# A decoder's first phase: 64-row transposes issued right behind the scores, projected and memory keys side by side in one tensor, and two of four softmax scalings moved from ScalarE to GpSimd

## The chip, the cores and the metric

The kernel runs on one core of one Trainium2 chip. The metric is the time of one execution in microseconds (us). Three runs of the kernel before took 1528.6, 1529.95 and 1530.91 us; the median, 1529.95 us, is what the change is compared with. One execution is also taken with the hardware profiler. The engines are called as the profile calls them: PE is TensorE's matmuls, PEld its weight loads, DVE is VectorE, ACT is ScalarE, POOL is GpSimd, SP is SyncE.

## The reference, cut to what matters

Input `x` is (32, 128, 128) in float32: 32 sequences of 128 rows with 128 features. Six residual blocks follow one another: a recurrent attention with 16 heads of 8, a cross attention with 16 heads of 64, a mixture of 8 experts with the best 2 chosen, a causal attention with normalised queries and keys, a banded cross attention, and a quantised linear layer. The change touches the second block only. In short:

```python
q = layernorm(x) @ wq + bq          # 16 heads of 64
k = concat(ctx @ wk + bk, mk)       # 128 projected keys, 128 memory keys
v = concat(ctx @ wv + bv, mv)
attn = softmax(q @ k.T / 8)         # 128 x 256 for each head
x = x + (attn @ v) @ wo + bo
```

The memory keys `mk` and values `mv` are the same for all sequences.

## The kernel before, in words

The program has three phases, one after the other on all engines: the first computes the recurrent attention, the cross attention and the routing; the second the experts; the third the last three blocks. Each engine has its own in-order program, written out by hand, and engines wait for each other on counting semaphores (`wait_ge`).

**The first phase is staged in slots.** All five programs loop over a slot number `s` from -53 to 152. Sequences are worked on in 8 groups of 4 (512 columns). The cross attention is cut into 128 **units**, one a slot from slot 0 on: a unit is one sequence and four heads (`hq` says which four of the 16), and 16 units make a group. `unit(i)` gives group, four heads and sequence. What belongs to one unit is spread over five slots:

- slot s: PE computes the scores (lines 744 and 746), 128 queries by 256 keys for each of four heads, into two PSUM banks. Two heads lie on the partitions 0 to 63, two on 64 to 127; a matmul has 64 rows of weights (queries) and streams keys, 128 projected ones from `KT` (tensor `kt_w2`), then 128 memory keys from `mkT`. DVE takes the negated maximum of the four heads (line 1122). ACT exponentiates each head into `pr` and sums it (line 950).
- slot s+1: DVE takes the reciprocals of the sums (line 1096, counted in semaphore `b_nd` when it is through) and scales heads 0 and 1 of `pr` in place (line 1099); ACT scales heads 2 and 3 (line 925, counted in `b_na`).
- slot s+2 (`LAG_PT`): PE transposes the eight 128x128 blocks of `pr` through full 128-row transposes (line 760) into banks 4 and 5, four blocks a bank; ACT copies each bank to `ptS` (line 934).
- slot s+3 (`LAG_PV`): PE multiplies with the values (line 898), 64 output partitions a head.
- slot s+4 (`LAG_OT`): ACT copies the result to `aoT` (line 917).

A float32 matmul appears as two instructions of equal shape, a transpose as one.

**What else a slot holds.** Every slot computes a chunk of the projected queries or keys (lines 852 and 857, with ACT copies in lines 1017 and 1021), and either a chunk of values (line 868, added to its bias by DVE in line 1081) or a part of the output projection (line 880, added to the residual by DVE in line 1088). Both of the latter go to bank 4, which the transposes of the next slot overwrite; so those transposes wait for that DVE addition (semaphores `b_v`, `b_add`), and the chunk waits for ACT's copy of bank 4 (`b_pts`). Bank 7 is shared by the steps of the recurrent attention and of the routing, of which most slots have one (table `BANK7`).

**GpSimd's queue** does one product of 128x512 in each of the slots 1 to 96 (lines 664 and 670, `KV`), always after it has waited for `b_nd`, that is for DVE's scaling in the same slot; also additions and products (lines 675, 677, 688), powers for the layer norms (line 352), and the indirect stores of routed rows (line 702). **DVE's order in a slot**: addition for the value or output chunk of the slot before, reciprocal, scaling, in some slots a scan (line 1068), the maximum (line 1122), then the steps of the recurrent attention and of the routing, many of them with two operands in SBUF (lines 1139, 1160, 1197 to 1200, 1235, 1243, 1313), and a scan in most odd slots. **ACT's order**: copy to `aoT`, scaling of heads 2 and 3, two copies to `ptS`, four exponentials, copies out of bank 7, the copy of the chunk.

## Time and profile before

| | |
|---|---|
| median of three runs | 1529.95 us (1528.6 to 1530.91) |
| the profiled execution's own time | 1531.66 us |
| its span, first to last instruction | 1529.7 us |
| busy: PE, PEld | 1362.8 us (89%), 1040.4 us (68%) |
| busy: DVE, ACT, POOL | 1148.0 us (75%), 1099.5 us (72%), 597.9 us (39%) |
| mean granted TensorE clock | 0.977 of full speed |
| units of the cross attention | scores start at 131.1 us (first unit) and 812 us (last) |

The page is read from the span down: busy shares of the engines, the span in forty slices, the chain of work that ended last, and the costliest groups of instructions. PE is the busiest engine, and matmul ends are modelled, so its share alone says little; the times between starts of matmuls say more.

### The profile page before, as it was taken

Reading aid. Unit: us, or ns where it says so; the run is one execution under the profiler, and the core shown is the slowest. Engines: PE = TensorE matmul, PEld = TensorE weight load, DVE = VectorE, ACT = ScalarE, POOL = GpSimd, SP = SyncE. Lnnn points to the kernel's source line nnn. Section 1 sums busy time; section 2 is a strip of 40 time slices with the busy share of each in tenths; the row PEclk is TensorE's granted clock in tenths of the full one; section 3 lists DMA queues with packets and bytes.
Section 4 is the critical chain, followed back from the end, with each engine's and each line's share of the span. In section 5 each row is a group of like instructions: output and inputs, shape, how many; then the busy total and the mean of one; then the engine's idle time right before and its main releaser. Section 6 shows DMA issues by size and latency. Waiting matters only on the chain.

```text
span 1529.7 us, 42924 instructions
## 1 busy us (share of the span) xinstructions
PE 1362.8 (89%) x15465; PEld 1040.4 (68%) x15465; DVE 1148.0 (75%) x2779; ACT 1099.5 (72%) x2899; POOL 597.9 (39%) x679
## 2 busy tenths in 40 slices
PE   2258999999999999999997699979889999999995
PEld 0124777777777777777776699957667777777763
DVE  3899879898898989786655444457778888787765
ACT  1126998898898898899995366657667877767763
POOL 0002333344443524330202635346754755544552
PEclk9999999999999999999999799989999999999997
DMA  6644141321423231102011333240000110000000
GB/s 171 154 112 104 43 105 36 90 63 37 108 53 89 58 81 46 50 15 77 15 36 49 87 98 87 58 141 18 20 23 25 25 38 10 23 23 3 23 9 15
DMA packets 82317, 88.63 MB, mean 58 GB/s; under 512 B 15296, under 2 KB 71488, under 8 KB 77504
## 3 DMA queue, kind: packets, MB, share of 16 engines
q1 hardware_dynamic: 74496, 73.65, 18.7%
q0 software_dynamic: 4096, 8.40, 1.9%
q10 hardware_dynamic: 3520, 3.84, 0.8%
q8 instruction: 130, 2.13, 0.6%
q14 instruction: 75, 0.61, 0.1%
HBM read 64.89 MB, written 17.83 MB: 54 GB/s over the span
## 4 chain that ended last, share of the span: by engine, by line
PE 65%; DVE 24%; issue 5%; ACT 3%; DMA 2%; ACTq 1%; POOL 1%; SPq 0%; DVEq 0%; POOLq 0%
PE P L898 7%; PE P L760 7%; PE P L1985 6%; PE P L744 5%; PE P L1481 4%; PE P L1514 4%; PE P L880 3%; DVE xnE L2310 3%; PE P L746 3%; PE P L868 3%; DVE qS L2310 3%; PE P L857 3%; PE P L852 3%; PE P L2003 3%; PE P L1947 2%
## 5 line engine op out<-in xcount | busy, mean ns | idle before, releaser
L950 ACT ACTIVATE pr<-P,nm 128x256 f32<-128x256 f32 x512 | 237.7, 489 | 9.7 <-DVE nm L1122 9.7
L1122 DVE TENSOR_REDUCE nm<-P 128x4 f32<-128x1024 f32 x128 | 156.1, 1220 | 46.7 <-PE P L746 46.5
L2194 ACT ACTIVATE et<-P 128x1024 f32<-128x1024 f32 x128 | 131.2, 1025 | 59.2 <-PE P L1992 59.0
L352 POOL TENSOR_TENSOR rstd<-ve,mhalf 128x1 f32<-128x1 f32 (+2 forms) x81 | 75.5, 936 | 225.9 <-DVE ve L347 225.3
L934 ACT COPY ptS<-P 128x512 f32<-128x512 f32 x256 | 136.8, 586 | 31.2 <-PE P L760 30.7
L760 PE MATMUL P<-ident,pr 128*128 128x128 f32 x1024 | 140.2, 280 | 5.5 <-DVE xb L1088 3.0
L925 ACT ACTIVATE pr<-pr,ri 128x256 f32<-128x256 f32 x256 | 118.9, 523 | 27.9 <-DVE pr L1099 26.6
L744 PE MATMUL P<-kt_w,qt 64*128 64x128 f32 x1024 | 126.7, 309 | 2.9 <-ACT pr L950 2.7
L760 PEld LDWEIGHTS P<-ident,pr 128*128 128x128 f32 x1024 | 110.3, 141 | 21.9 <-issue 8.6
L1573 ACT ACTIVATE hT<-P,mixing 128x128 f32<-128x128 f32 x284 | 81.4, 369 | 60.5 <-PE P L1481 60.5
L664 POOL TENSOR_TENSOR kv_qk<-kv_qk,r_w 128x512 f32<-128x512 f32 x48 | 61.1, 1272 | 161.9 <-DVE pr L1099 115.7
L670 POOL TENSOR_TENSOR kv_qk<-kv_qk,mixing 128x512 f32<-128x512 f32 x48 | 61.1, 1273 | 154.1 <-DVE pr L1099 154.1
L746 PE MATMUL P<-mkT,qt 64*128 64x128 f32 x1024 | 113.9, 272 | 0.0
L2310 DVE TENSOR_REDUCE qS<-P 128x8 f32<-128x1024 f32 x64 | 78.2, 1222 | 46.8 <-PE P L1985 46.4
L950 ACT ACTIVATION_READ_ACCUMULATOR pr<-P,nm 128x1 f32 x512 | 112.9, 220 | 0.0
L744 PEld LDWEIGHTS P<-kt_w,qt 64*128 64x128 f32 x1024 | 91.7, 185 | 28.0 <-issue 26.0
L2310 DVE TENSOR_REDUCE xnE<-P 128x8 f32<-128x1024 f32 x64 | 78.4, 1225 | 40.3 <-PE P L1985 39.3
L898 PE MATMUL P<-ptS,V 128*64 128x128 f32 x1024 | 106.7, 287 | 0.0
L898 PE MATMUL P<-ptS,mv 128*64 128x128 f32 x1024 | 100.0, 274 | 0.0
L898 PEld LDWEIGHTS P<-ptS,V 128*64 128x64 f32 x1024 | 58.1, 137 | 55.3 <-issue 40.7
L1902 POOL TENSOR_SCALAR_AFFINE_SELECT et<-et 128x1024 f32<-128x1024 f32 x64 | 71.0, 1109 | 61.1 <-ACT et L2194 60.6
L746 PEld LDWEIGHTS P<-mkT,qt 64*128 64x128 f32 x1024 | 92.3, 188 | 0.0
(355 smaller groups left out, 3929.2 us busy)
## 6 DMA issues: line engine op xcount, KB each, us to landing
kv_qk<-scr_v SPq DMA_DIRECT2D x16, 1024.0 KB, 8.1
r_w<-scr_r SPq DMA_DIRECT2D x16, 1024.0 KB, 10.5
xt<-scr_xs SPq DMA_DIRECT2D x71, 64.0 KB, 1.8
scr_ys<-yt SPq DMA_DIRECT2D x71, 64.0 KB, 1.5
x<-in_x SPq DMA_DIRECT2D x8, 256.0 KB, 9.8
scr_v<-mixing SPq DMA_DIRECT2D x8, 256.0 KB, 2.0
scr_r<-mixing SPq DMA_DIRECT2D x8, 256.0 KB, 2.0
xb<-in_x SPq DMA_DIRECT2D x8, 256.0 KB, 4.3
```

The source lines that it names most:

```text
L744: nc.tensor.matmul(bank[:, cc * KEYS:cc * KEYS + T], q, KT[part, c, b * T:(b + 1) * T], start=True, stop=True)
L746: m = nc.tensor.matmul(bank[:, cc * KEYS + T:(cc + 1) * KEYS], q, mkT[part, c, :], start=True, stop=True)
L760: m = nc.tensor.transpose(P[:, 4 + kb, h * T:(h + 1) * T], pr[:, i % 3, h * KEYS + kb * T:h * KEYS + (kb + 1) * T], ident[:, :])
L898: m = nc.tensor.matmul(P[64 * hh:64 * hh + 64, 6, cc * T:(cc + 1) * T], src, ptS[:, i % 2, (kb * 4 + h) * T:(kb * 4 + h + 1) * T], start=( ...
L925: m = nc.scalar.activation(t, t, ACT.Copy, scale=ri[:, i % 3, h:h + 1])
L934: nc.scalar.copy(ptS[:, i % 2, kb * 512:(kb + 1) * 512], P[:, 4 + kb, :])\
L950: e = nc.scalar.activation(pr[:, s % 3, h * KEYS:(h + 1) * KEYS], scores(s)[:, h // 2, (h % 2) * KEYS:(h % 2 + 1) * KEYS], ACT.Exp, bias=n ...
L1122: nc.vector.tensor_reduce(nm[:, s % 3, 0:4].rearrange("p (a h) -> p a h", a=2), scores(s).rearrange("p a (h k) -> p a h k", k=KEYS), AX.X, ...
L1573: m = nc.scalar.activation(hT[:, t % 3, c, :], P[:, 2 + t % 2, c * 128:(c + 1) * 128], ACT.Gelu, bias=b1[:, bass.ds(e1 + c, 1)])
L1985: return nc.tensor.matmul(scores[:, k, a, :], q[part, a, cols], keys[part, a, cols], start=False, stop=(a == 3))
L2194: nc.scalar.activation(et[:, u % 4, :, :, :], scoresT, ACT.Exp).then_inc(S["h_exp"], 1)
L2310: nc.vector.tensor_reduce(q[:, b, :, DH].rearrange("p (a r k) -> p r k a", r=2, k=2)[:, r], scores, AX.X, ALU.max, negate=True).then_inc(S ...
```

## The change

Three things. The projected keys and the memory keys stand side by side in one tensor, 640 columns for each pair of heads, so that one matmul streams 256 columns through a strided pattern (the keys of sequence b and the memory keys). The transposes work on 64 partitions each, sixteen in place of eight, with a moving identity of 64 columns; the lower 64 queries go to bank 4, the upper ones to bank 5, and ACT's two copies write with a stride. The scaling of heads 2 and 3 moves from ACT's program to POOL's, ahead of the products, and waits there for `b_ri`, which DVE raises after head 0. The sizes of the other tensors and the number of DMAs stay as they were.

```diff
-        r8_w1, kt_w2, qt = [sb_shared(n, E * F) for n in ("r8_w1", "kt_w2", "qt")]
+        r8_w1, qt = [sb_shared(n, E * F) for n in ("r8_w1", "qt")]
+        kt_w2 = sb_shared("kt_w2", 8 * (N + MEM))
...
-            mkT = sb1("mkT", [128, 8, MEM])
...
-            KT = kt_w2.rearrange("p (c n) -> p c n", n=N)
+            KT = kt_w2.rearrange("p (c n) -> p c n", n=N + MEM)
+            mkT = KT[:, :, N:N + MEM]
...
@@ pool_program
                 for s in range(FIRST, LAST + 16):
+                    i = s - 1
+                    if 0 <= i < UNITS:
+                        pool.wait_ge(S["b_ri"], i + 1)
+                        for h in range(2, 4):
+                            t = pr[:, i % 3, h * KEYS:(h + 1) * KEYS]
+                            m = nc.gpsimd.tensor_scalar(t, t, ri[:, i % 3, h:h + 1], None, ALU.mult)
+                        m.then_inc(S["b_na"], 1)
...
@@ tensor_program, scores
                             for hh in range(2):
-                                bank = scores(s)[:, hh, :]
                                 part, c = slice(64 * hh, 64 * hh + 64), 2 * hq + cc
-                                q = QT[part, c, b * T:(b + 1) * T]
-                                nc.tensor.matmul(bank[:, cc * KEYS:cc * KEYS + T], q, KT[part, c, b * T:(b + 1) * T],
-                                                 start=True, stop=True)
-                                m = nc.tensor.matmul(bank[:, cc * KEYS + T:(cc + 1) * KEYS], q, mkT[part, c, :],
-                                                     start=True, stop=True)
+                                keys = KT[part, c, :].rearrange("p (m k) -> p m k", k=T)[:, b:GS + 1:GS - b, :]
+                                m = nc.tensor.matmul(scores(s)[:, hh, cc * KEYS:(cc + 1) * KEYS], QT[part, c, b * T:(b + 1) * T],
+                                                     keys, start=True, stop=True)
                         m.then_inc(S["b_s"], 1)
...
@@ tensor_program, transposes
                         for kb in range(2):
                             for h in range(4):
-                                m = nc.tensor.transpose(P[:, 4 + kb, h * T:(h + 1) * T],
-                                                        pr[:, i % 3, h * KEYS + kb * T:h * KEYS + (kb + 1) * T],
-                                                        ident[:, :])
-                            m.then_inc(S["b_pt"], 1)
+                                k = 4 * kb + h
+                                for half in range(2):
+                                    part = slice(64 * half, 64 * half + 64)
+                                    m = nc.tensor.transpose(P[:, 4 + half, 64 * k:64 * k + 64],
+                                                            pr[part, i % 3, h * KEYS + kb * T:h * KEYS + (kb + 1) * T],
+                                                            ident[part, part])
+                                    if k == 7:
+                                        m.then_inc(S["b_pt"], 1)
...
@@ scalar_program
-                    i = s - 1
-                    if 0 <= i < UNITS:
-                        act.wait_ge(S["b_ri"], i + 1)
-                        for h in range(2, 4):
-                            t = pr[:, i % 3, h * KEYS:(h + 1) * KEYS]
-                            m = nc.scalar.activation(t, t, ACT.Copy, scale=ri[:, i % 3, h:h + 1])
-                        m.then_inc(S["b_na"], 1)
...
-                        for kb in range(2):
-                            act.wait_ge(S["b_pt"], 2 * i + kb + 1)
-                            nc.scalar.copy(ptS[:, i % 2, kb * 512:(kb + 1) * 512], P[:, 4 + kb, :])\
-                              .then_inc(S["b_pts"], 1)
+                        for half in range(2):
+                            act.wait_ge(S["b_pt"], 2 * i + half + 1)
+                            nc.scalar.copy(ptS[:, i % 2, :].rearrange("p (k q) -> p k q", q=T)[:, :, 64 * half:64 * half + 64],
+                                           P[:, 4 + half, :].rearrange("p (k q) -> p k q", q=64)).then_inc(S["b_pts"], 1)
```

## Rows read from the trace of the kernel before

**Rows 1.** Stretches: length; PE, PEld, DVE, ACT, POOL busy; clock; DMA share, GB/s.

```profile
484.23:574.41 90.18, 89.38 (x816) 67.11 (x814) 77.88 (x180) 80.33 (x239) 35.75 (x29) 1.00 0.27 69
...
574.41:661.96 87.55, 85.57 (x805) 65.06 (x803) 73.71 (x173) 76.47 (x233) 33.32 (x27) 1.00 0.16 41
...
661.96:745.38 83.42, 83.42 (x795) 64.01 (x793) 59.39 (x155) 75.60 (x230) 12.67 (x12) 1.00 0.15 43
```

**Rows 2.** PE's waits, 130 to 818 us: total, times, longest.

```profile
PE P L760 <- DVE xb L1088: 3.0, 4, 1.7
...
PE P L744 <- ACT pr L950: 2.7, 3, 1.4
```

**Rows 3.** PE's timeline through one slot: start, length, what, count.

```profile
672.34 0.50 PE L744 MATMUL P<-kt_w,qt 64*128 64x128 f32 x4
...
673.11 0.49 PE L746 MATMUL P<-mkT,qt 64*128 64x128 f32 x4
...
673.54 1.09 PE L760 MATMUL P<-ident,pr 128*128 128x128 f32 x8
...
674.47 1.02 PE L857 MATMUL P<-xTb,wq 128*128 128x512 f32 x2
...
675.33 1.05 PE L880 MATMUL P<-wo,aoT 128*128 128x128 f32 x8
...
677.33 0.39 PE L744 MATMUL P<-kt_w,qt 64*128 64x128 f32 x2
```

**Rows 4.** PE's timeline where matmuls stream 8 columns only.

```profile
721.46 0.96 PE L825 MATMUL P<-rw,tT 128*128 128x8 f32 x8
```

**Rows 5.** PEld's timeline, same slot: output projection's first load.

```profile
674.92 0.19 PEld L880 LDWEIGHTS P<-wo,aoT 128*128 128x128 f32 x1 [0.26 <-ACT ptS L934]
```

**Rows 6.** By line and shape, 110 to 800 us: busy, mean ns.

```profile
L925 ACT ACTIVATE pr<-pr,ri 128x256 f32<-128x256 f32 x244 | 113.4, 524 | 26.2 <-DVE pr L1099 24.8
...
L1180 DVE TENSOR_REDUCE hn<-r_w 128x64 f32<-128x512 f32 x7 | 4.7, 676 | 0.0
```

**Rows 7.** DVE's waits, 484.3 to 574.4 us: first and last of six.

```profile
DVE nm L1122 <- PE P L746: 6.1, 8, 1.1
...
DVE ri L1096 <- ACT pr L950: 0.2, 1, 0.2
```

**Rows 8.** DVE's waits, 495.47 to 545.80 us, both of them.

```profile
DVE nm L1122 <- PE P L746: 0.8, 1, 0.8
...
DVE xb L1206 <- PE P L804: 0.6, 1, 0.6
```

**Rows 9.** DVE's, then POOL's timeline in a slot of that stretch.

```profile
513.61 0.62 DVE L1099 TENSOR_SCALAR pr<-pr,ri 128x256 f32<-128x256 f32 x2
...
514.14 1.22 DVE L1122 TENSOR_REDUCE nm<-P 128x4 f32<-128x1024 f32 x1
...
515.28 0.85 DVE L1197 TENSOR_TENSOR r_w<-r_w,gnw 128x512 f32<-128x512 f32 x1
...
516.16 0.69 DVE L1198 TENSOR_TENSOR r_w<-r_w,gnb 128x512 f32<-128x512 f32 x1
...
514.32 1.27 POOL L670 TENSOR_TENSOR kv_qk<-kv_qk,mixing 128x512 f32<-128x512 f32 x1 [2.15 <-DVE pr L1099]
```

**Rows 10.** DVE's, then POOL's timeline in an earlier slot.

```profile
192.44 1.63 DVE L1099 TENSOR_SCALAR pr<-pr,ri 128x256 f32<-128x256 f32 x2
...
192.51 1.41 POOL L688 TENSOR_TENSOR xb<-xb,bias 128x512 f32<-128x512 f32 x1
```

**Rows 11.** POOL's instructions by line and shape, whole run.

```profile
L1902 POOL TENSOR_SCALAR_AFFINE_SELECT et<-et 128x1024 f32<-128x1024 f32 x64 | 71.0, 1109 | 61.1 <-ACT et L2194 60.6
...
L1897 POOL TENSOR_SCALAR_AFFINE_SELECT et<-et 128x512 f32<-128x512 f32 x64 | 43.2, 674 | 78.7 <-ACT et L2194 78.1
...
L1924 POOL COPY vE<-ctk 128x128 f32<-128x128 f32 x32 | 9.8, 308 | 0.0
...
L670 POOL TENSOR_TENSOR kv_qk<-kv_qk,mixing 128x512 f32<-128x512 f32 x48 | 61.1, 1273 | 154.1 <-DVE pr L1099 154.1
```

More of the change, by code:

```diff
@@ L647, in sync_program @@
                             e0, e1 = half * E // 2, (half + 1) * E // 2
-                            sp.dma_start(units_of(kt_w2)[:, e0 * FC:e1 * FC, :],
+                            sp.dma_start(units_of(kt_w2[:, 0:E * F])[:, e0 * FC:e1 * FC, :],
                                          d["w2T"].rearrange("(u f) h -> f u h", f=128)[:, e0 * FC:e1 * FC, :])\
@@ L1016, in scalar_program @@
                             act.wait_ge(S["b_kp"], 8 * g + c + 1)
-                            nc.scalar.activation(KT[:, c, :], P[:, 3, :], ACT.Identity, bias=bqk[:, 1, c:c + 1])\
+                            nc.scalar.activation(KT[:, c, 0:N], P[:, 3, :], ACT.Identity, bias=bqk[:, 1, c:c + 1])\
                               .then_inc(S["b_k"], 1)
@@ L1349, in sb2 @@
                 return own.enter_context(nc.sbuf_tensor(name, shape, dt))
-            w1, w2, b1, b2 = r8_w1, kt_w2, mixing[:, 0:E * D], mixing[:, 8 * N:8 * N + E * D]
+            w1, w2, b1, b2 = r8_w1, kt_w2[:, 0:E * F], mixing[:, 0:E * D], mixing[:, 8 * N:8 * N + E * D]
             qS, kS, vD, xb, ya, yb, xnD, xTd, qkv, qkq, hn3 = homes
```

## The prediction

> **What bounds the kernel now.** I read the windows first, one for each group of sixteen slots. A steady group takes 90.2 us with PE busy 89.4, ACT 80.3, DVE 77.9 and POOL 35.8, at the full clock [rows 1]; the last groups with less side work keep PE as full and leave DVE idle. PE's waits come next: while the 128 units run, its matmuls wait little, most of it for DVE's addition out of bank 4 (3.0 us) and for ACT's exponentials (2.7 us) [rows 2]. So PE's own stream paces most slots. The timeline of one slot says what it is made of: 4.99 us from scores to scores, 1.20 of it from the first score to the first transpose, 0.93 the eight transposes, 0.86 a chunk of two 512-column instructions [rows 3]. Last, DVE's waits: in a steady group they total 9.6 us [rows 7], but in the nine slots from 495.47 to 545.80 us only 1.4 us [rows 8]. There DVE is a second bound, close under PE, and what is added to it there is paid in time.
>
> **The change, part by part.** The sum is made against the profiled execution's 1531.66 us, 1.7 above the median, and carried over to the median as it is.
>
> *Scores.* Sixteen instructions of 128 columns become eight of 256. They run two at a time, on the two halves of the rows, as the counts and lengths show: sixteen starts in 1.20 us, while a stream of 512 columns takes 0.43, so one of 128 takes 0.107 and sixteen in a row would take 1.71 [rows 3]. The streaming is the same 0.86 after the change (four times 0.215). Now the last score starts 0.99 after the first (673.60, where the last group ends, less 0.27, the length of one) and streams until 1.10. After: 0.1 for the first weight load, then 0.86 and 0.01 of offset, 0.97. That is 0.12 less; nothing less is the other bound, since the same columns flow.
>
> *Transposes.* Eight pairs of 64-row transposes with 64 moving columns stream half as long, but each still loads 128 columns of weights. The price of such a load shows where matmuls stream only 8 columns: eight starts within 0.96 less 0.25 of length, hence one every 0.11 us although nothing is streamed [rows 4]. Pairs of loads run side by side in the scores. So eight pairs take 8 x 0.11, what eight transposes take today; only the last one's stream is shorter, 0.05. Between scores and transposes PE idles today some 0.15 (1.20 less 1.10, and the second transpose late); after, the rows of scores and transposes match, but the chunk behind them uses all 128, so I move the gap and credit nothing. The Trainium skill, "TensorEngine Tiling (Array Packing)", section Key Properties, says that changing the tiling mode drains the engine; by that rule too the number of drains a slot is unchanged. The same page, section Theoretical Speedup, gives up to 2x for a dimension of 64 or less; that would be 0.44 a slot and is a rival below.
>
> Both together: **0.17 us a slot**, bounds 0.05 and 0.32 (the gap gone as well).
>
> *Two halves complete together.* ACT's first copy starts after the fourth transpose today and after the last pair then, 0.44 later; 0.27 is given back because the transposes begin that much earlier (0.12 and the gap), 0.05 by the shorter stream. PE's load for the output projection waited for that copy until 674.92, 0.4 before its matmul at 675.33 [rows 3, 5]. It moves to 675.04 and the matmul to 675.16: just in time, so zero, covered by the 0.86 of the chunk. If ACT were late, every microsecond would show.
>
> *ACT* loses two activations a slot, 2 x 0.52 [rows 6]. It was not the bound: zero. Its earlier exponentials may give back part of the 2.7 that PE waits for exponentials [rows 2]; I take none, the end is -2.7. The strided writes of the copies move as many elements: zero. SP's program issues the same DMAs.
>
> *POOL* gets two scalings of 128x256 in each slot, in front of its product and in front of everything else of that slot. One-source operations cost 0.67 for 512 and 1.11 for 1024 elements, a copy of 128 costs 0.31; the two-source product 1.27 for 512 [rows 11]. The two sizes make 0.24 to start and 0.22 for 256 elements, 0.46; from the copy it is 0.31 + 0.11 = 0.42. I take **p = 0.43**, nearer the copy, the closest in length; the ends are 0.34 (half of the 0.67) and 0.72 (the two-source product, 0.64 in proportion, with a start). The Trainium skill, "GPSIMD Engine Reference", section Elementwise — side-by-side cycle accounting, gives 1.8 cycles an element as the best case of a loop of several operations; by that figure, as an estimate, a scaling would be 0.38 and a start, 0.62, and the sum that of the slower rival. PE needs the scaled heads a slot later, some 4 us. POOL is busy 2.2 us of 5.6 a slot [rows 1] and 3.1 then, so that wait costs nothing. The new wait, on `b_ri`, ends before today's wait on `b_nd`, so what is queued behind it (the product, powers, indirect stores) is held up by the two scalings alone.
>
> *But POOL and DVE block each other.* In a tight slot POOL's product ends at 515.59, and DVE's product with two SBUF operands, begun at 515.28, takes 0.85 where the equal one behind it takes 0.69 [rows 9]. In an earlier slot one of two scalings on DVE, 0.62 together elsewhere, waits out POOL's addition: 1.63 [rows 10]. The maximum, which reads PSUM, runs beside POOL at its 1.22. Today the product starts right behind DVE's scaling and lies almost wholly under that maximum; only 0.16 sticks out. Afterwards two scalings come first. The start of the first is hidden behind DVE's scaling (0.14, as in that earlier slot, where 1.41 less 0.28 of waiting leaves 1.13 for a 1.27), so the product ends 2p - 0.30 = **0.56 later**, and a DVE instruction with two SBUF operands or a scaling behind the maximum waits that much longer. The Trainium skill, "SBUF — State Buffer", section Who interferes with whom, calls this an exclusive lock held for the whole instruction; the trace agrees, 0.85 against 0.69.
>
> In the nine tight slots two have a 0.68 reduction [rows 6] behind the maximum, which needs no lock: free. Seven pay 0.56, 3.9 in all. DVE has 1.4 of waits there to absorb, and about 0.4 of lateness at either end. So the stretch, 50.3 us, grows by **2.1**. In the other seven slots DVE waits over 1 us each and PE's gain holds: -1.2. A steady group: **+0.9**.
>
> **The sum.** Four steady groups +3.6. The first, and the one at 574 us where DVE is 4 us less busy [rows 1], half way between the full gain of -2.7 and +0.9: -0.9 each, -1.8. The 31 slots from 662 us on, where POOL has no products and DVE idles: 31 x 0.17 = -5.3. Total -3.5: 1531.66 becomes 1528.2, and the median 1529.95 becomes **1526.4**. PE gains some 21 us, of which DVE takes 18 back.
>
> **The rivals.**
>
> *The block costs nothing extra* (products slip into later gaps, or POOL scales in well under 0.4): 127 x 0.17 = 21.6, less about 2 that DVE cannot follow in the tight slots: -19, 1511. For it: DVE waits 9.6 us a group. Against: they lie elsewhere [rows 8]. Chance 0.22. *The transposes halve*, to 0.44 a slot: 0.44 more in the 31 free slots, -14, while elsewhere DVE caps the gain; 1512. Against it is the 0.11 of a load [rows 4]. Chance 0.03. This is what the Trainium skill's "TensorEngine Tiling (Array Packing)" would give.
>
> *Slower: POOL's scaling is dear.* Place: the queue of POOL between DVE's scaling and the product. At p = 0.60 the product ends 0.90 later; fourteen of sixteen slots become tight, DVE's 80.5 us of own time a group (90.2 less 9.6) [rows 1, 7] grows to 93.1, +2.9 and, as the slots cannot even each other out, up to +4. Times four, +12 to +16; the two light groups +1 each; the end -5.3: +9 to +13, 1541. At 0.72: 80.5 + 14 x 1.14 = 96.5, +6.3 a group, +3 in the light ones, +26 in all, 1556. It decides from p = 0.49, where the sum crosses zero. For it: a scaling reads a scalar for each partition, which no row of POOL does. Chance 0.25.
>
> *The pairs don't overlap in transpose mode*: 16 x 0.11 in place of 8, +0.88 - 0.17 = 0.7 a slot, 127 slots, +90, 1620. Against: the same loads overlap in the scores. Chance 0.03.
>
> *It does not do what it says*: merged keys bring nothing, only the 0.05 is left, and the block stays. A steady group +2.1 - 0.35, times four +7; the light ones +0.5 each; the end -1.6: +6.4, 1536. Chance 0.05.
>
> **How the numbers follow.** The likeliest, 0.42, has its own range 1520 to 1533 (p from 0.40 to 0.49, 0.05 to 0.17 a slot). A measurement of this kernel can tell about 0.2%, 3.1 us, from no change: 1526.9 to 1533.0. Of the 0.42, 0.27 falls below and 0.14 within. Faster: 0.27 + 0.22 + 0.03 = 0.52. Same: 0.14. Slower: 0.01 + 0.25 + 0.03 + 0.05 = 0.34. Range 1508 to 1549: it holds the first two rivals, the last and most of the third, and leaves out p near 0.72 and the missing overlap, some 0.12.
>
> **What would show it.** In the profile after: a slot without side work late in the phase (672 us) at 4.82 in place of 4.99; scores to transposes under 1.0 us; transposes one pair every 0.11; a pause before the chunk instead of before the transposes. POOL's scaling with mean near 0.43, in 256 instructions. DVE busy higher by some 15 to 25 us with no instruction added, on the lines behind the maximum (1197, 1160, 1139, 358, 1235); DVE's waits gone from all steady groups; PE's waits for 1088 and 1081 up from 4 us to over 10. ACT busy down by about 120. I am wrong if the steady groups run shorter than 89 us (no block), or over 92 (dear scaling), or if the late slots don't shorten.

## The result and the profile after

The changed kernel takes 1560.49 us (median of four runs, 1559.58 to 1561.76) beside 1530.30 of the kernel before (with a fourth run) on the same chip: a ratio of 1.020, 95% interval 1.018 to 1.022. It is 30 us slower, where 1526.4 was forecast, and outside the range of 1508 to 1549. The profiled execution has a span of 1557.7 us where the kernel before had 1529.7.

I read the windows first, group by group of sixteen units; columns as in [rows 1]. Two steady groups, the light group, and the last 31 units:

```profile
414.30:512.30 98.00, 84.67 (x816) 57.31 (x814) 93.86 (x193) 67.41 (x207) 70.79 (x62) 1.00 0.26 64
512.30:609.40 97.10, 85.51 (x816) 58.27 (x814) 90.01 (x180) 67.32 (x207) 68.58 (x61) 0.98 0.25 63
609.40:704.10 94.70, 82.23 (x806) 56.68 (x804) 84.15 (x175) 63.99 (x201) 66.00 (x59) 0.98 0.15 38
704.10:847.00 142.90, 138.66 (x1506) 101.66 (x1504) 103.30 (x264) 115.58 (x372) 79.77 (x83) 1.00 0.13 39
```

A steady group went from 90.2 us to 97 to 98. In the one at 512.30, which has the 180 instructions of DVE of the one shown of before, PE is busy 4 us less, DVE 12 us more and POOL 33 us more. The last 31 units run the other way, 142.9 us where they had taken 155.3. From the starts of the scores: units 0 to 96 take 574.0 us (530.9 before), 96 to 127 142.9 (155.3), and what is behind the last unit 710.7 (712.4). So +43.1, -12.4 and -1.7, and 1.1 less ahead of the first unit: together the 28 us between the spans.

PE's waits from 130 to 847 us, columns as in [rows 2]; then DVE's:

```profile
PE P L768 <- issue: 30.5, 33, 1.6
PE P L768 <- DVE xb L1089: 29.4, 31, 2.6
PE P L768 <- DVE V L1082: 6.8, 4, 1.9
```

```profile
DVE kv_qk L1069 <- POOL kv_qk L678: 14.4, 11, 1.8
...
DVE kv_qk L1314 <- POOL kv_qk L672: 10.1, 7, 1.8
```

PE waited 3.0 us for DVE's addition into xb [rows 2]; now it is 29.4, and at the same matmul (the transposes) 30.5 us end with no releaser shown. DVE has become the bound: it is busy 93.9 of the 98.0 us from 414.30 on. Its waits for POOL are new, 24.5 us in all and 7.7 in the three groups that are looked at closely below; there its 564 instructions take 277.6 us where they took 238.8, so most of its lateness is longer instructions and not waiting. POOL's scaling and product, by line and shape (columns as in [rows 11]):

```profile
L663 POOL TENSOR_SCALAR pr<-pr,ri 128x256 f32<-128x256 f32 x256 | 250.6, 987 | 238.0 <-DVE pr L1100 237.5
...
L678 POOL TENSOR_TENSOR kv_qk<-kv_qk,mixing 128x512 f32<-128x512 f32 x48 | 62.5, 1303 | 0.0
```

(The first mean, 987 ns, takes in scalings that were held up; the median of that line is 0.95 us.) One slot of the stretch shows it, DVE's timeline, then POOL's (start, length):

```profile
439.86 0.33 DVE L1100 TENSOR_SCALAR pr<-pr,ri 128x256 f32<-128x256 f32 x1
440.11 1.21 DVE L1069 TENSOR_TENSOR_SCAN kv_qk<-mixing,kv_qk 128x512 f32<-128x512 f32 x1
441.25 1.19 DVE L1123 TENSOR_REDUCE nm<-P 128x4 f32<-128x1024 f32 x1
442.36 0.21 DVE L384 SCALAR_TENSOR_TENSOR hn<-hn 128x64 f32<-128x64 f32 x1
442.61 0.22 DVE L386 TENSOR_TENSOR hn<-hn 128x64 f32<-128x64 f32 x1
442.86 1.34 DVE L387 SCALAR_TENSOR_TENSOR hn<-hn 128x64 f32<-128x64 f32 x1
444.24 0.23 DVE L384 SCALAR_TENSOR_TENSOR hn<-hn 128x64 f32<-128x64 f32 x1
```

```profile
440.04 2.84 POOL L663 TENSOR_SCALAR pr<-pr,ri 128x256 f32<-128x256 f32 x2 [0.20 <-DVE pr L1100]
442.86 1.27 POOL L672 TENSOR_TENSOR kv_qk<-kv_qk,r_w 128x512 f32<-128x512 f32 x1
```

The product used to start right behind DVE's scaling and lay under the maximum [rows 9]. Now it starts at 442.86, when the maximum is over, and DVE's 128x64 operation at 442.86 lasts 1.34 us, until POOL's product ends, instead of 0.23. The two operations ahead of it ran beside POOL's *scaling* at their usual length. In this slot DVE's scan kept the first scaling back as well, as it does in 12 slots. Over the 48 slots from 316.5 to 609.4 us the product starts 1.66 us behind DVE's scaling (median; 0.08 in the kernel before) and ends 1.79 us behind the maximum (0.10 before).

What a DVE instruction takes over the lower tenth of its line and shape in that run I call its excess. An excess of 0.08 us or more I call a stall, and give it to the POOL instruction that it overlaps most. In the three groups from 316.5 to 609.4 us, with 48 slots, the excess is 51.1 us: 40 stalls beside POOL's products make 39.2 of it (0.98 each), five beside its scalings 0.8. In the same groups of the kernel before the excess is 9.9 us in all.

### The profile page after: what moved, and what is told of

Its sections match the earlier page's. It is cut to its first block, busy times and chain, and to the rows that moved or that the text cites. A ratio compares the mean times of both kernels' runs of the same rounds, so it can differ in the third digit from the quotient of the medians.

```text
span 1557.7 us, 42924 instructions
## 1 busy us (share of the span) xinstructions
PE 1324.1 (85%) x15465; PEld 968.0 (62%) x15465; DVE 1214.4 (78%) x2779; ACT 995.1 (64%) x2643; POOL 853.0 (55%) x935
## 4 chain that ended last, share of the span: by engine, by line
PE 38%; DVE 36%; issue 12%; POOL 9%; ACT 3%; DMA 1%; ACTq 1%; SPq 0%; DVEq 0%; POOLq 0%
PE P L1986 6%; PE P L1482 4%; PE P L1515 4%; DVE nm L1123 4%; POOL pr L663 4%; DVE xnE L2311 3%; DVE qS L2311 3%; PE P L751 2%; PE P L2004 2%; PE P L907 2%; DVE kv_qk L1069 2%; PE P L1948 2%; PE P L2103 2%; DVE st L338 2%; PE P L768 1%
## 5 line engine op out<-in xcount | busy, mean ns | idle before, releaser
L663 POOL TENSOR_SCALAR pr<-pr,ri 128x256 f32<-128x256 f32 x256 | 250.6, 987 | 238.0 <-DVE pr L1100 237.5
L751 PE MATMUL P<-kt_w,qt 64*128 64x256 f32 x1024 | 145.2, 402 | 4.7 <-ACT pr L951 4.5
L768 PE MATMUL P<-ident,pr 64*128 64x64 f32 x2048 | 89.9, 227 | 67.6 <-issue 30.5
L768 PEld LDWEIGHTS P<-ident,pr 64*128 64x128 f32 x2048 | 80.9, 140 | 102.4 <-issue 98.6
L951 ACT ACTIVATION_READ_ACCUMULATOR pr<-P,nm 128x1 f32 x512 | 109.2, 213 | 0.0
L1069 DVE TENSOR_TENSOR_SCAN kv_qk<-mixing,kv_qk 128x512 f32<-128x512 f32 x64 | 80.2, 1253 | 15.1 <-POOL kv_qk L678 14.4
L889 PEld LDWEIGHTS P<-wo,aoT 128*128 128x128 f32 x512 | 68.0, 196 | 35.6 <-ACT ptS L935 22.8
L1100 DVE TENSOR_SCALAR pr<-pr,ri 128x256 f32<-128x256 f32 x256 | 84.9, 373 | 4.5
L1898 POOL TENSOR_SCALAR_AFFINE_SELECT et<-et 128x512 f32<-128x512 f32 x64 | 43.1, 673 | 78.7 <-ACT et L2195 78.1
```

What stands on the lines that cost most here:

```text
L663: m = nc.gpsimd.tensor_scalar(t, t, ri[:, i % 3, h:h + 1], None, ALU.mult)
L751: m = nc.tensor.matmul(scores(s)[:, hh, cc * KEYS:(cc + 1) * KEYS], QT[part, c, b * T:(b + 1) * T], keys, start=True, stop=True)
L768: m = nc.tensor.transpose(P[:, 4 + half, 64 * k:64 * k + 64], pr[part, i % 3, h * KEYS + kb * T:h * KEYS + (kb + 1) * T], ident[part, part])
L951: e = nc.scalar.activation(pr[:, s % 3, h * KEYS:(h + 1) * KEYS], scores(s)[:, h // 2, (h % 2) * KEYS:(h % 2 + 1) * KEYS], ACT.Exp, bias=n ...
L1069: nc.vector.tensor_tensor_scan(KV[:, j, :], dec[:, :], KV[:, j, :], 0.0, ALU.mult, ALU.add)\
L1100: m = nc.vector.tensor_scalar(t, t, ri[:, i % 3, h:h + 1], None, ALU.mult)
```

## The experiments

The experiments ran on several chips, and each is compared by its ratio to the kernel before on its own chip. That kernel took 1553.15 us beside the first four experiments below, 1556.53 beside the product first, the unscaled heads, the fill and the one tensor_tensor ahead, 1530.95 beside the one behind, the head on each engine and the two prices, and 1552.95 beside the last three. A steady group's length below is a third of the three groups from unit 32 to unit 80, at 0.98 to 1.00 of the clock.

### Which part does it

**The scaling back on ACT**, all else as changed:

```diff
@@ pool_program: the seven lines removed
@@ scalar_program
+                    i = s - 1
+                    if 0 <= i < UNITS:
+                        act.wait_ge(S["b_ri"], i + 1)
+                        for h in range(2, 4):
+                            t = pr[:, i % 3, h * KEYS:(h + 1) * KEYS]
+                            m = nc.scalar.activation(t, t, ACT.Copy, scale=ri[:, i % 3, h:h + 1])
+                        m.then_inc(S["b_na"], 1)
```

> The changed kernel with the scaling of heads 2 and 3 back on ACT; scores, transposes and copies stay as changed. Theory A (the whole loss comes from GpSimd's two scalings, 0.93 us each, in front of its product; the PE part is a gain of 0.47 us a slot, as the slots from 672 us on show, 4.99 before and 4.52 after): PE's stream of a steady group falls from 90.2 to about 82, but ACT is busy 80.3 us of it and becomes the bound near 84 to 86; with 31 late slots this gives 1485 to 1505 us. Rival B (the halves that complete together and the strided copies delay ACT and PE by themselves, so that the PE part costs too): 1530 us or more, with ACT waiting for transposes as long as in the changed kernel (176 us).

Measured 0.981 (0.979 to 0.983), steady group 86.1 us: theory A.

**The scaling on POOL alone**: the kernel before with the mirror of that diff.

> The kernel before with nothing changed but the scaling of heads 2 and 3, moved from ACT to GpSimd. Theory A: all of the loss is here, and none of the gain: slots up to 96 as in the changed kernel (43 us more than before) or a little less, the 31 late slots as before, so 1565 to 1580 us. Rival B: 1530 to 1545 us. Theory C (GpSimd is slow, but DVE loses time only because PE's shorter slots press it): 1530 to 1550 us too, with DVE's operations not longer than before.

Measured 1.021 (1.019 to 1.023), a steady group of 98.1 us, bare late slots of 4.99 and 4.96 as before. Alone it costs as much as the whole change. That is theory A but for its size (1565 us would be a ratio of 1.023). Rival B is out, and so is theory C: with PE's slots as long as before, DVE's excess in the three groups is 50.4 us.

**Merged keys alone** (the kernel before with the one tensor of keys and four matmuls, eight instructions, of 256 columns), and **64-row transposes alone** (with the sixteen transposes and the strided copies):

> The kernel before with the merged keys alone: old 128-row transposes, old copies, scaling on ACT. Theory A: from the timelines, first score to the end of the score stream is 0.97 us in place of 1.10, the pause before the transposes stays: 0.1 to 0.13 us a slot less, 10 to 16 us in all, 1514 to 1520 us. If the merged keys bring nothing: 1528 to 1532 us.

> The kernel before with the 64-row transposes and their copies alone: separate keys, scaling on ACT. Theory A: pairs of 64-row transposes start every 0.062 us as in the changed kernel, 0.50 in place of 0.87 a slot, 0.35 to 0.4 us less, 30 to 45 us in all where neither DVE nor ACT ends the slot: 1488 to 1510 us. My recorded working had a pair every 0.11: then 1522 to 1530 us. Rival B: slower than before.

Measured 0.993 (0.991 to 0.994) and 0.989 (0.987 to 0.990). The bare late slot goes from 4.99 to 4.86 and to 4.65 us: 0.13 and 0.34. They add to the 0.47 of both (4.52): theory A in both, by the slot. The ratios multiply to 0.981, which is that of both with ACT's scaling. By the whole times, PE's parts are worth 1.9%, and POOL's scaling takes 3.9% back. Those times may understate the parts, though. In the traces of these three kernels some slots behind unit 96 are much longer than their neighbours, and the units 96 to 127 take 161.2, 163.6 and 157.8 us where the kernel before, in its trace on another chip, took 155.3 with longer bare slots. That may be what keeps the transposes alone above the 0.972 to 0.987 that theory A meant; more of it under "A train of stores". The steady groups have no such slot: 90.1 us before, 88.9 with the keys, 87.2 with the transposes, 86.1 with both.

### The scaling itself, or what stands behind it

**The product first**: POOL's seven lines behind the two products of the slot instead of ahead of them.

```diff
@@ pool_program
-                    i = s - 1
-                    if 0 <= i < UNITS:
-                        pool.wait_ge(S["b_ri"], i + 1)
...
                     for j in range(DH if s > 0 else 0):
...
+                    i = s - 1
+                    if 0 <= i < UNITS:
+                        pool.wait_ge(S["b_ri"], i + 1)
...
                     g = group_at(s, -41)
```

> The changed kernel, with POOL's two scalings of a unit placed behind the KV product of the same slot instead of ahead of it; POOL's work is the same. Theory A (each scaling takes 0.94 us and holds back the operations of DVE that read and write SBUF beside it; DVE's 0.5 to 0.8 us more per unit are the loss): the order changes nothing in the sum, the steady group of 16 units stays at 94 to 99 us and the ratio to the kernel before at 1.01 to 1.025. Theory B (the scalings are only in the way of the product, and DVE's scan and product wait for it, 14.4 us as recorded and the rest through the order of DVE's queue): the waits for POOL go, the steady group falls to 86 to 91 us and the ratio to 0.98 to 0.995.

Measured 0.983 (0.981 to 0.984), a group of 89.9 us: theory A, with 1.01 to 1.025, fell, and theory B has both numbers. The same scalings, 1.07 us each in this trace, cost 3.7% less in another place of the queue. DVE's timeline, then POOL's:

```profile
511.07 1.21 DVE L1123 TENSOR_REDUCE nm<-P 128x4 f32<-128x1024 f32 x1
512.21 0.84 DVE L1198 TENSOR_TENSOR r_w<-r_w,gnw 128x512 f32<-128x512 f32 x1
513.09 0.85 DVE L1199 TENSOR_TENSOR r_w<-r_w,gnb 128x512 f32<-128x512 f32 x1
513.97 0.88 DVE L1201 TENSOR_TENSOR r_w<-r_w,mixing 128x512 f32<-128x512 f32 x1
```

```profile
511.24 1.26 POOL L671 TENSOR_TENSOR kv_qk<-kv_qk,mixing 128x512 f32<-128x512 f32 x1 [0.43 <-DVE pr L1100]
512.48 2.27 POOL L677 TENSOR_SCALAR pr<-pr,ri 128x256 f32<-128x256 f32 x2
```

The product is under the maximum again. DVE's additions beside the scalings take 0.85 instead of 0.69, 0.16 each, and the scalings 1.14 each; neither holds the other for its whole length.

**No scaling of heads 2 and 3**: that part of the computation is left out, with the waits for it. **A fill in its place**: the same, but POOL fills a 128x256 tile five times where the scalings stood.

```diff
@@ pool_program, in the scalings' place (the second kernel only)
+                        for k in range(5):
+                            if i or k:
+                                pool.wait_ge(S["b_na"], 5 * i + k)
+                            nc.gpsimd.memset(junk[:, :], 0.0).then_inc(S["b_na"], 1)
```

> The changed kernel without any scaling of heads 2 and 3 and without the two waits for it (that part of the computation is left out); DVE scales heads 0 and 1 as before. It is the most that moving the scaling off ACT could bring. Theory A (PE is the bound once POOL's scalings are gone, as in the kernel with the scaling on ACT): the steady group takes 84 to 86.5 us, and the ratio is 0.975 to 0.982, hardly better than 0.981 with ACT. Theory B (ACT, at 79 us of 86 busy with the scaling, also sets the pace there): 80 to 83 us and 0.960 to 0.970.

> As the kernel without scaling of heads 2 and 3 (that part is left out), but POOL fills a small tile of 128x256 five times in the scalings' place, some 0.3 to 0.4 us each with the wait between them, 1.6 to 2.0 us together: POOL's product is as late as in the changed kernel, but no operation of POOL reads SBUF meanwhile. Theory A (an operation of POOL that reads and writes SBUF holds DVE's back; one that only writes doesn't): DVE's additions of constants in SBUF take 0.70 us again and not 1.66, the steady group 84 to 89 us, ratio 0.975 to 0.99. Theory B (the late product is the loss): 94 to 98 us and 1.01 to 1.02. If a fill holds DVE too, the group is as long as theory B says, but DVE's busy time is up again by 11 us per group, which tells the two apart.

Measured 0.979 (0.977 to 0.980), as theory A has it, and 1.010 (1.008 to 1.012), theory B. A delay of the product that reads nothing and computes nothing costs 3.1%, and more where the products are: units 0 to 96 take 506.2 us without the fill and 565.4 with it. (The kernel without has long slots behind unit 96, 155.3 us in place of 144.3, which hide some of it.) One group of each by windows, the one without, then the one with the fill:

```profile
380.60:466.30 85.70, 82.62 (x816) 57.80 (x814) 80.30 (x193) 67.40 (x207) 37.53 (x30) 1.00 0.30 75
```

```profile
410.00:506.50 96.50, 86.09 (x818) 57.84 (x816) 92.24 (x193) 67.77 (x207) 66.55 (x110) 0.98 0.26 65
```

DVE is busy 12 us more with the same 193 instructions. The last sentence of the expectation takes this as the sign of a fill that holds DVE; the timeline says that it is not the fill. DVE's, then POOL's:

```profile
443.97 0.68 DVE L1196 TENSOR_TENSOR r_w<-r_w,gnw 128x512 f32<-128x512 f32 x1
444.69 1.74 DVE L1197 TENSOR_TENSOR r_w<-r_w,gnb 128x512 f32<-128x512 f32 x1
446.46 0.69 DVE L1199 TENSOR_TENSOR r_w<-r_w,mixing 128x512 f32<-128x512 f32 x1
```

```profile
442.72 1.93 POOL L665 MEMSET junk<- 128x256 f32 x5 [1.27 <-DVE pr L1098]
444.62 1.26 POOL L679 TENSOR_TENSOR kv_qk<-kv_qk,mixing 128x512 f32<-128x512 f32 x1
```

The addition beside the fills (443.97) takes 0.68; the one begun just after the product has started takes 1.74. In three groups 40 stalls of 35.8 us lie beside the products, 0.6 us beside the fills.

**One tensor_tensor for both heads**, ahead of the product as in the changed kernel, and **behind it**:

```diff
-                        for h in range(2, 4):
-                            t = pr[:, i % 3, h * KEYS:(h + 1) * KEYS]
-                            m = nc.gpsimd.tensor_scalar(t, t, ri[:, i % 3, h:h + 1], None, ALU.mult)
-                        m.then_inc(S["b_na"], 1)
+                        t = pr[:, i % 3, 2 * KEYS:4 * KEYS].rearrange("p (h k) -> p h k", h=2)
+                        nc.gpsimd.tensor_tensor(t, t, bcast(ri[:, i % 3, 2:4], 2, KEYS), ALU.mult).then_inc(S["b_na"], 1)
```

> The changed kernel, with heads 2 and 3 scaled by one tensor_tensor of POOL over 128x512 (the two sums broadcast along the keys) instead of two tensor_scalar of 128x256 at 0.94 us each. Theory A (the price of the scalings is the loss): like POOL's other products of 128x512 this takes 1.27 to 1.31 us, 0.6 us less per unit, and the steady group falls from 97.5 to 88 to 91 us (16 x 0.57 = 9 us less), 0.985 to 0.995 of the kernel before. Theory B (it is that POOL has the scaling at all ahead of its product, whatever it takes): 93 to 98 us, a ratio of 1.005 to 1.02.

> The kernel with the product first, with the two scalings behind it in one tensor_tensor of 128x512, which took 1.07 us where two tensor_scalar take 1.87. Theory A (what POOL's scaling still costs there is its length: 94.5% of the gain of the kernel with ACT's scaling): the steady group falls from 90 to 86.5 to 88.5 us, the ratio to before is 0.974 to 0.981, under both the kernel with the product first and the one that scales on ACT. Theory B (it is POOL's tensor_tensor that holds back the operation of DVE that starts beside it, and its tensor_scalar does not, as the 40 stalls beside the products and the 5 beside the scalings in three groups of the changed kernel say): the scaling now stalls DVE by 0.5 to 1 us a unit, the steady group takes 92 to 98 us and the ratio is 0.990 to 1.01.

Measured 0.995 (0.993 to 0.997) and 1.000 (0.999 to 1.001). Ahead of the product the shorter operation delays it less (it starts 0.86 us behind DVE's scaling, median): 92.9 us a group instead of 97.6. That lies between the two theories, 88 to 91 and 93 to 98. Behind the product it is *worse* than two tensor_scalar that take 0.8 us longer together: 93.1 us against 89.9. Theory B there holds: beside POOL's tensor_tensor DVE has 59 stalls in three groups, 31.8 us or 0.54 each, where beside the two tensor_scalar it has 71, 13.6 us or 0.19 each.

**One head on ACT, one on POOL** (behind the product, one tensor_scalar a unit), with a semaphore of its own for ACT's half:

```diff
@@ pool_program, behind the products
+                        for h in range(3, 4):
...
@@ scalar_program, where the scalings had stood
+                        act.wait_ge(S["b_ri"], i + 1)
+                        t = pr[:, i % 3, 2 * KEYS:3 * KEYS]
+                        nc.scalar.activation(t, t, ACT.Copy, scale=ri[:, i % 3, 2:3]).then_inc(S["b_nc"], 1)
```

> The kernel with the product first, with head 2 scaled on ACT and head 3 on POOL behind the product (one tensor_scalar of 0.92 us). Theory A (POOL's scaling beside DVE costs by its length): the steady group falls from 90 to 87 to 88.5 us and the ratio to 0.976 to 0.981. Theory B (the second scaling is outside the stretch that matters; only the first one, up against the operations that follow the maximum, costs): 89 to 91 us and 0.981 to 0.985.

Measured 0.978 (0.977 to 0.979), 1496.99 us beside 1530.95: theory A. A group takes 87.0 us.

The excess of DVE in the three groups, and a group's length, side by side:

| kernel | DVE's excess, us | group, us |
|---|---|---|
| heads 2 and 3 not scaled | 11.5 | 85.8 |
| scaling on ACT | 11.6 | 86.1 |
| one head each, product first | 18.1 | 87.0 |
| two scalings, product first | 28.9 | 89.9 |
| one tensor_tensor ahead | 40.2 | 92.9 |
| one tensor_tensor, product first | 42.6 | 93.1 |
| fill ahead | 46.9 | 96.3 |
| one tensor_scalar of 128x512 ahead (next section) | 48.5 | 95.4 |
| changed kernel | 51.1 | 97.6 |

The order of the one is the order of the other, but for the last two before the changed kernel, 0.9 us a group apart. From the second row to the last the excess grows by 13.2 us a group and the group by 11.5.

### Two prices measured by themselves

**One tensor_scalar of 128x512** that multiplies heads 2 and 3 both by head 2's sum (head 3's own sum is left out):

> The changed kernel, with one tensor_scalar of POOL over 128x512 that multiplies heads 2 and 3 both by head 2's sum (head 3's own sum is left out), to measure the price of the operation by size. Theory A (it is paid by the element, 256 columns in 0.92 us): 1.75 to 1.85 us, and the kernel takes as long as the changed one, 1.01 to 1.02 of before. Theory B (most of the 0.92 us is a fixed start): 1.1 to 1.4 us, under the 1.07 to 1.27 us of tensor_tensor or near it, and 0.99 to 1.00 of before.

```profile
L662 POOL TENSOR_SCALAR pr<-pr,ri x128: 1564/1592/2587, 134.7 to 840.3; 128x512 f32<-128x512 f32 x128
```

(Least, median and greatest ns.) The median is 1.59 us for 512 elements where 256 take 0.92 to 0.95: some 0.65 for each 256 elements and 0.3 to start, between the two theories and a little nearer the first. The kernel took 1548.94 us in one run beside 1530.95, 1.012, as theory A has it.

**Both transposes of a pair on rows 0 to 63** (rows 64 to 127 are left out, the others transposed twice): `part = slice(0, 64)` in the transposes.

> The changed kernel, with both transposes of each pair reading rows 0 to 63 (rows 64 to 127 of the scores are left out, the first half is transposed twice), so that no two neighbours use different halves of the array. Theory A (a pair starts every 0.062 us because its two halves load and run beside each other): the 16 transposes take 16 x 0.062 = 1.0 us or more instead of 0.50, and the bare late slot 5.0 us or more instead of 4.51. Theory B (a load of 64 rows takes half the time of one of 128 rows, 0.055 us, whatever half it goes to, and half of a pair is hidden): 16 x 0.03 to 0.04 us, 0.5 to 0.65 us, and a bare slot of 4.5 to 4.7 us.

PE's timeline in a bare late slot, of this kernel, then of the changed one:

```profile
822.85 1.15 PE L768 MATMUL P<-ident,pr 64*128 64x64 f32 x16
823.93 1.12 PE L866 MATMUL P<-xTb,wq 128*128 128x512 f32 x2
```

```profile
785.83 0.81 PE L751 MATMUL P<-kt_w,qt 64*128 64x256 f32 x6
786.48 0.66 PE L768 MATMUL P<-ident,pr 64*128 64x64 f32 x16
787.07 1.12 PE L861 MATMUL P<-ctP,wk 128*128 128x512 f32 x2
```

Sixteen starts take 0.93 us (822.85 to 823.78, one every 0.062) instead of 0.50, and the bare slot 5.01 instead of 4.52: theory A. (The kernel took 1578.38 us in one run, 1.031 of before.) Each half starts a transpose every 0.062 us, and two halves do it at once.

### A train of stores

The kernel with ACT's scaling had two odd slots in its late part, 10.4 and 11.8 us among neighbours of 4.5 to 6, which the changed kernel hasn't. Merged keys alone (10.2 us), transposes alone (8.9 and 15.0) and the unscaled heads (12.3) have them too. So three more, on one chip: that kernel again, the one with a head on each engine again, and that with ACT's scaling with POOL waiting for the reciprocals at the top of each slot and nothing behind the wait:

```diff
@@ pool_program
                 for s in range(FIRST, LAST + 16):
+                    if 0 <= s - 1 < UNITS:
+                        pool.wait_ge(S["b_ri"], s)
```

> The kernel with the scaling back on ACT once more, to stand on one chip with the two others of this call. Theory A (its two odd slots, 5.9 and 7.3 us over the 4.5 of their neighbours, in which ACT waits for nothing the semaphores explain while POOL issues eight indirect stores 1.27 us apart, come from the kernel): they are there again near 650 and 727 us, and the ratio is 0.978 to 0.983. Theory B (they belong to the chip of that call): they are gone, 96 to 127 takes 143 to 145 us, and the ratio is 0.970 to 0.975.

> The kernel with the product first and one head scaled on ACT, one on POOL, once more beside the others: 0.976 to 0.980 by both theories, with no odd slot, since POOL's wait for the reciprocals spaces the stores two to a slot.

> The kernel with the scaling on ACT, and a wait of POOL for the unit's reciprocals at the top of each slot, with no work behind it, so that its indirect stores come two to a slot as in the changed kernel. Theory A (the train of eight stores is what holds up the fetch of ACT's instructions): no slot from 96 to 127 over 6 us, that stretch takes 143 to 146 us in place of 157.8, and the ratio is 0.970 to 0.975, the fastest of all. Theory B (the odd slots have another cause): they stay or the stretch is as in the run beside it, and the ratio is that of the kernel with the scaling on ACT, within 0.2%.

Measured 0.982 (0.980 to 0.983), 0.976 (0.974 to 0.977) and 0.976 (0.974 to 0.977): theory A for the first and for the last, though not quite the 0.970 to 0.975 that it gave the last, which is level with a head on each engine and not the fastest of all. The odd slots are there again in the first (9.9 and 11.7 us), not in the others; units 96 to 127 take 157.1, 143.1 and 146.3 us. ACT's timeline in the second odd slot of the first kernel, then POOL's, two of eight stores that start 1.27 us apart:

```profile
732.73 1.07 ACT L936 COPY ptS<-P 128x512 f32<-128x512 f32 x2 [5.81 <-remote]
```

```profile
728.04 0.96 POOL L703 DMA_INDIRECT scr_xs<-xnC,slot_in  x1 [0.31 <-issue]
729.30 0.96 POOL L703 DMA_INDIRECT scr_xs<-xnC,slot_in  x1 [0.30 <-issue]
```

and POOL's in the paced kernel:

```profile
724.19 0.96 POOL L705 DMA_INDIRECT scr_xs<-xnC,slot_in  x1 [0.30 <-issue]
726.70 0.96 POOL L705 DMA_INDIRECT scr_xs<-xnC,slot_in  x1 [1.54 <-DVE pr L1103]
727.96 0.96 POOL L705 DMA_INDIRECT scr_xs<-xnC,slot_in  x1 [0.30 <-issue]
731.89 0.96 POOL L705 DMA_INDIRECT scr_xs<-xnC,slot_in  x1 [2.98 <-DVE pr L1103]
```

ACT stands for 5.8 us with its transposes long done and no semaphore late ("remote" is what the profile prints when it finds no releaser on this core). Spaced stores, with no work added, take the stall away. The train by itself is not enough, though. The kernel before, traced on a chip where it takes 1530 us, has the same trains of eight and no odd slot; ACT's row, then POOL's:

```profile
752.31 1.07 ACT L934 COPY ptS<-P 128x512 f32<-128x512 f32 x2 [0.44 <-PE P L760]
```

```profile
751.61 0.96 POOL L702 DMA_INDIRECT scr_xs<-xnC,slot_in  x1 [0.30 <-issue]
752.87 0.96 POOL L702 DMA_INDIRECT scr_xs<-xnC,slot_in  x1 [0.30 <-issue]
```

All five traces with odd slots come from chips where that kernel takes 1553 us or more, and no trace shows the kernel before on such a chip; so whether the chip or the kernel makes the difference is open, and with it how much of the odd slots the ratios of these kernels contain. That it is the fetch of ACT's instructions that comes late was only argued. In the first run of this kernel the DMA queue for instructions moved a packet in each of the two stretches, but it moves one every 12.6 us (median) in the kernel before too, one of them at 750.4 us, within the train that did no harm.

For the change itself this comparison says most: with both heads left on ACT and the stores spaced the ratio is 0.976, with one head moved to POOL 0.976 as well, and the group is 86.5 us against 87.3. All of the gain is PE's part; moving the scaling bought nothing.

## Why the prediction was wrong

**The mechanism was right and its price was not.** The likeliest case and the slower rival were the same chain: two scalings ahead of the product, the product out from under the maximum, and whatever DVE does next waits for its end. This is what the fill and the product put first have shown. In the terms of the sum: the four steady groups grew by 28.6 us where it had 3.6, the first group and the one at 574 us by 14.5 where it had -1.8, and the 31 late slots fell by 12.4 where it had 5.3. The term that failed is p. I took 0.43 us from POOL's one-source rows, which have 0.24 to start and 0.22 for 256 elements [rows 11]. A tensor_scalar with a scalar for each partition has 0.3 to start and 0.65 for 256: the start was right, the slope a third of what it is, and p is 0.92 to 0.95. I had set the upper end at 0.72, from the two-source product; that is a different operation, near only in that it has a second input. In "for it: a scaling reads a scalar for each partition, which no row of POOL does" the doubt stood, and a bound from both sides should have reached past 0.72 for it.

*"The product ends 2p - 0.30 later"* gives 1.56 at the measured p; behind the maximum it ends 1.69 later (1.79 against 0.10), so the formula was nearly right. In the slot above the product starts 2.82 after the first scaling did, since DVE's scan kept the scalings back once more, and it held DVE 1.1. Most slots pay: 40 stalls of 0.98 in 48, where I had seven of sixteen at 0.56. A stall beside a product is 1.12 us at most in the three groups, less than the product's 1.27; the formula has no such limit. "Over 92: dear scaling" was the test, and 97 to 98 is its answer. The rival's own 1556 at p = 0.72 lay 4.5 us from the truth, and stood outside my range; but that it came so near is partly luck. At p = 0.93 its own working gives 80.5 + 14 x 1.56, or 102.3 us a group, where 97 to 98 was measured, and the late slots gave back 7 us more than it had.

*The Trainium skill's figures.* From the Trainium skill, "GPSIMD Engine Reference", section Elementwise — side-by-side cycle accounting, I had 0.38 and a start, an estimate of 0.62. By the measured slope, 0.65 without the start, its best case is too low here too, though nearer than my rows. The Trainium skill, "SBUF — State Buffer", section Who interferes with whom, has the first to issue block the other for its whole instruction, and has a DVE operation with two SBUF inputs left alone by a POOL instruction that only writes. For POOL's tensor_tensor and for the fills the traces agree (1.34 and 1.74 us beside the one, 0.68 beside the other). For POOL's tensor_scalar they do not: DVE's additions beside it take 0.85 against 0.69, and the scalings 1.14 against 0.92, so neither has it whole.

*Scores*: 0.12 forecast, 0.13 measured alone; scores to transposes 0.97 forecast, 0.968 measured.

*Transposes*: 0.05 forecast, 0.34 measured alone. "Each still loads 128 columns of weights", at 0.11 [rows 4], is the step that failed: that row is a load of 128 rows, and one of 64 rows starts every 0.062 us. So eight pairs take 0.50, not 0.88, and the rival "the transposes halve", with 0.03 of the chances and 0.44 a slot, was close (0.50 where the eight took 0.87). This is why the late slots gained 12.4 us where I had 5.3. That rival was right on the transposes and wrong on the total of 1512, since the dear scaling took more than they gave.

*ACT*: "zero" nearly holds. ACT's busy time went from 1099.5 to 995.1 us, but in the kernel with nothing scaled the group is only 0.3 us shorter than with ACT's scaling. *PE's waits for DVE* went up, as forecast, to 36 us instead of "over 10"; *DVE's busy time* by 66 us instead of 15 to 25. *The lines*: of those that I named behind the maximum, 358 and 1235 stall, and behind 1139 and 1197 it is the next one that does; other lines stall as well. *The pause* moved before the chunk, as forecast: 0.15 us from the last transpose's start to the chunk's, 0.09 more than a transpose takes.

**What was missed altogether** is that the order of POOL's queue is free. The change puts the scalings ahead of the product though nobody needs them before the next slot; the prediction costed that place and never asked what another place would cost.

## What to carry to other kernels

When work moves to an engine that shares a resource with the bound, look less at its own length than at what is queued behind it: here a product of 1.27 us was nearly free under a reduction out of PSUM and cost about 1 us in 40 slots of 48 as soon as it slid out. Put what others wait for, or what has a free place, first, and what is needed a slot later behind it; that alone turned 1.020 into 0.983, and a head on each engine gave 0.976 to 0.978, faster than both kernels. Ask first whether the move is needed at all: with ACT's scaling left where it was and the stores spaced, the ratio was 0.976 too. And take an operation's price only from a row of the same operation with the same kinds of operands, or widen the bounds well past the nearest one.

## What the runs showed of the hardware

- POOL's tensor_scalar with a scalar for each partition: 0.92 to 0.95 us for 128x256, 1.59 for 128x512 (f32). Its tensor_tensor with the scalar broadcast does 128x512 in 1.08 us, a third less, but the stalls of DVE beside it are 0.54 us long where those beside two tensor_scalar are 0.19.
- In the changed kernel DVE's scan holds POOL's tensor_scalar, and not the other way round: beside the scan the first of two scalings takes 1.93 us instead of 0.92 (the pair 2.84), in 12 slots, while the scan takes its usual 1.21 to 1.22.
- A 64-row transpose of 64 moving columns starts every 0.062 us on each half of the rows, both halves at once; a 128-row one every 0.11 us.
- Eight indirect stores of POOL 1.27 us apart came with stalls of ACT of 3 and 6 us that no semaphore explains, on a chip where the kernel before takes 1553 us; the same stores two to a slot came with none there. In the kernel before, on a chip where it takes 1530 us, the same eight came with none.
